# A 65th column of zeros for V's low part, so that all weighing matmuls have one width

## What is computed

```
q = einsum('bsd,dhk->bshk', x, Wq) + bq        # B=2, S=2048, D=256, H=16, K=64
k = einsum('bsd,dhk->bshk', x, Wk) + bk
v = einsum('bsd,dhk->bshk', x, Wv) + bv
scores = einsum('bqhk,bshk->bhqs', q, k) / sqrt(K)
attn = softmax(scores, axis=-1)
ctx = einsum('bhqs,bshk->bqhk', attn, v)
y = x + einsum('bqhk,hkd->bqd', ctx, Wo) + bo
```

## Time and profile before

| | |
|---|---|
| median of 3 runs | 2787.41 us (2786.87 to 2787.42) |
| the profiled execution | 2788.39 us, its span 2786.6 us |
| TensorE | 97% busy, 34,176 matmuls |
| ScalarE | 88% busy |
| VectorE | 84% busy |
| GpSimd | 82% busy |
| first to last weighing matmul | 75.3 to 2415.4 us |

### The profile page before, as it was taken

The page is one execution under the profiler, slowest core; times in us unless marked ns, Lnnn a source line. Parts: engine busy times, 40 slices in busy tenths (PEclk is TensorE's granted clock), DMA queues, the critical chain, the costliest instruction groups (busy, mean ns, idle before and its releaser), DMA issues. The chain is left out here.

```text
span 2786.6 us, 83179 instructions
## 1 busy us (share of the span) xinstructions
PE 2692.4 (97%) x34176; PEld 1723.9 (62%) x34176; DVE 2343.3 (84%) x4203; ACT 2446.4 (88%) x4760; POOL 2274.3 (82%) x1919
## 2 busy tenths in 40 slices
PE   6999999999999999999999999999999999889997
PEld 3566666666666666656666666666666666656664
DVE  6888888999988998768888888898998898578775
ACT  5999999999999999889999999999999999856553
POOL 4898989999999998789899999999999999613233
PEclk9999999999999999999999999999999999999998
DMA  4222222111122222122222122221222212221210
GB/s 133 48 55 57 55 56 73 42 36 35 37 42 42 42 42 42 23 87 55 57 55 53 40 45 42 42 42 42 42 42 42 42 40 83 81 76 46 91 54 23
DMA packets 207100, 144.89 MB, mean 52 GB/s; under 512 B 157824, under 2 KB 181632, under 8 KB 206720
## 3 DMA queue, kind: packets, MB, share of 16 engines
q1 hardware_dynamic: 206720, 139.58, 20.8%
HBM read 51.20 MB, written 37.88 MB: 32 GB/s over the span
## 5 line engine op out<-in xcount | busy, mean ns | idle before, releaser
L554 POOL TENSOR_TENSOR p_l<-p_f,p_h 128x512 f16<-128x512 f32 x1536 | 1946.1, 1295 | 91.0 <-ACT p_h L628 88.2
L681 DVE TENSOR_REDUCE mx<-ps_aux 128x1 f32<-128x512 f32 x2048 | 1349.3, 681 | 298.6 <-PE ps_aux L855 291.3
L627 ACT ACTIVATE p_f<-ps_score 128x512 f32<-128x512 f32 x2048 | 1272.6, 623 | 17.6 <-PE ps_score L884 17.5
L628 ACT ACTIVATE p_h<-ps_score 128x512 f16<-128x512 f32 x2048 | 1283.5, 628 | 0.0
L909 PEld LDWEIGHTS ps_ctx<-v_hi_one_lo,p_h 128*128 128x128 f16 x16384 | 891.3, 97 | 244.9 <-POOL p_l L554 1.2
L909 PE MATMUL ps_ctx<-v_hi_one_lo,p_h 128*128 128x65 f16 (+1 forms) x16384 | 920.9, 194 | 1.1 <-POOL p_l L554 1.0
L909 PE MATMUL ps_ctx<-v_hi_one_lo,p_l 128*128 128x65 f16 x8192 | 791.3, 192 | 0.0
L883 PE MATMUL ps_score<-q_hilo,k_hihi 128*128 128x512 f16 x2048 | 776.9, 379 | 4.7 <-ACT p_h L628 3.4
L884 PE MATMUL ps_score<-q_hi_max,k_lo_one 65*128 65x512 f16 x2048 | 778.6, 380 | 0.0
L855 PE MATMUL ps_aux<-k_hihi,q_hilo 128*128 128x512 f16 x2048 | 621.7, 382 | 15.2 <-DVE xTl L760 7.2
L699 DVE TENSOR_TENSOR p_l<-p_f,p_h 128x512 f16<-128x512 f32 x512 | 538.4, 1052 | 18.6 <-ACT p_h L628 18.6
(11 more groups left out here) (186 smaller groups left out, 2155.2 us busy)
## 6 DMA issues: line engine op xcount, KB each, us to landing
v_heads<-v_new SPq DMA_DIRECT2D x64, 258.0 KB, 2.0
v_hi_one_lo<-v_heads SPq DMA_DIRECT2D x32, 516.0 KB, 6.1
heads<-ctx_n SPq DMA_DIRECT2D x128, 128.0 KB, 2.0
x_all<-heads SPq DMA_DIRECT2D x8, 2048.0 KB, 9.1
k_hihi<-hi_st SPq DMA_DIRECT2D x62, 256.0 KB, 4.4
q_hi_max<-hi_st SPq DMA_DIRECT2D x32, 256.0 KB, 3.5
k_lo_one<-lo_st SPq DMA_DIRECT2D x32, 256.0 KB, 4.3
q_hilo<-hi_st SPq DMA_DIRECT2D x31, 256.0 KB, 3.2
```

What stands on the lines that cost most here:

```text
L554: nc.gpsimd.tensor_tensor(p_l[:, r], p_f[:, r], p_h[:, r], ALU.subtract).then_inc(lo_pool, 1)
L627: nc.scalar.activation(p_f[:, r], ps_score[:, bank], ACT.Exp, scale=exp_scale)
L628: nc.scalar.activation(p_h[:, r], ps_score[:, bank], ACT.Exp, scale=exp_scale).then_inc(exp_done, 1)
L681: nc.vector.reduce_max(mx[:, blk % 2, tt, ch:ch + 1], ps_aux[:, n % SIDE], AX_X).then_inc(max_read, 1)
```

## The change

V's rows get a 130th element, always zero, so that the low part is 65 columns wide as well. The middle matmul of a query tile reads it and writes all 65 columns of the tile's place; the last of them gets zero added. The tiles and the scratch tensor grow by this column (rows of 260 bytes for 258), and VectorE sets the zeros once, at the start. The order of all work, the semaphores and the number of matmuls and DMAs stay.

```
-    VW = 2 * K + 1
+    VW = 2 * K + 2
...
-        V = [sb(f"v_hi_one_lo{u}", [P, KT, VW], F16) for u in range(2)]
+        V = [sb(f"v_hi_one_lo_zero{u}", [P, KT, VW], F16) for u in range(2)]
...
-                nc.gpsimd.tensor_tensor(v_new[:, n % 4, :, K + 1:VW], v_wide[:, n % 2].rearrange("p (h k) -> p h k", k=K),
+                nc.gpsimd.tensor_tensor(v_new[:, n % 4, :, K + 1:VW - 1], v_wide[:, n % 2].rearrange("p (h k) -> p h k", k=K),
                                         v_new[:, n % 4, :, 0:K], ALU.subtract).then_inc(v_ready, 1)
...
             nc.vector.memset(v_new[:, :, :, K:K + 1], 1.0)
+            nc.vector.memset(v_new[:, :, :, VW - 1:VW], 0.0)
...
                     v_one, v_lo = V[u][:, kt, 0:K + 1], V[u][:, kt, K + 1:VW]
-                    parts = [(acc, p_h, v_one), (acc[:, 0:K], p_h, v_lo), (acc, p_l, v_one)]
+                    parts = [(acc, p_h, v_one), (acc, p_h, v_lo), (acc, p_l, v_one)]
...
-    v_scratch = nc.dram_tensor("v_heads", (B, P, S // P, wqk.shape[1], wqk.shape[2] + 1), F16, kind="Internal").ap()
+    v_scratch = nc.dram_tensor("v_heads", (B, P, S // P, wqk.shape[1], wqk.shape[2] + 2), F16, kind="Internal").ap()
```

## The result

| | before | after |
|---|---|---|
| median, 12 runs each | 2787.19 us | 2794.01 us |
| lowest to highest | 2784.54 to 2788.85 | 2792.67 to 2794.94 |
| the profiled execution | 2788.39 us | 2793.41 us |
| its span | 2786.6 us | 2791.6 us |
| first to last weighing matmul | 2340.1 us | 2346.4 us |

The changed kernel is slower: ratio 1.0024, 95% interval 1.0017 to 1.0032, or 6.8 us between the medians. The forecast was 34 us faster, and the time lies outside the range.

The account below looks back on a forecast made before the run. TensorE's own matmul stream was taken as the bound. 31 heads at 1.126 us gave 34.9, less 1 for waits: 34 us off the profiled 2788.39, so 2754.4, or 2753.5 us for the median; range 2746 to 2790.

Parts of the forecast that it names:

- What bounds the kernel: Attention heads: TensorE's own stream sets the pace in 31 heads, 70.8 us a plain head; ScalarE in the last.
- The cost of a 65-column matmul: Weighing stream: 29.0 ns from starts in the longest run, taken as 29.2, leaving 4.4 ns of stall a narrow matmul.
- p_l x2: Timeline group of two 65-column low-probability matmuls, last of one query tile and first of the next; 29.0 ns each.
- the stall: Extra time at each query tile's 64-column middle matmul, taken as 4.4 ns, 8192 times: 36.0 us.
- What is left is its width: Middle matmul: its 64-column width causes the stall, so 65 columns remove it; gain 34 us, chance 0.62.
- The upper end: Middle matmul: the stall stays and a column is added, 0.4 ns at 2.4 GHz or 0.8 by pairs.
- rival 3: Tile's column 64: waiting for the column just written stalls both steps within a tile; 36 us more, 2823, chance 0.07.
- its small form: Middle matmul: the stall stays and the 65th column costs 0.8 ns; 6.7 us more, 2794, chance 0.04.
- Rival 1: Middle matmul: the stall comes with reading V's low part, not the width, and stays; 2787 to 2791, chance 0.20.
- Rival 4: Middle matmul: 64 columns are a cheaper class that the 65th leaves, stall still on top; 2828, chance 0.01.
- The side edits: VectorE's zero memset hidden, V's longer rows about 0.04 us on the first load, GpSimd's row step no cost.
- Rival 5: Plain heads: another engine takes over if it needs over 69.7 us; could cost some us; no separate chance.

Follow-up runs that it names:

- e3: Changed kernel with the middle matmul reading V's high part and the ones again, V's low part left out of the sum; 2779.1 us, ratio 0.9966.
- e6: Kernel before with rows of 136 elements and the low part at element 72, so both parts start on 16 bytes; 2779.5 us, ratio 0.9972.
- e17: Kernel before's widths, rows of 144 elements, high part at element 2, low part at 74, all starts 4 bytes past a 16-byte boundary; 2777.1 us, ratio 0.9962.
- e18: Kernel before's widths, rows of 144 elements, high part at element 1, low part at 73, all starts 2 bytes past a 16-byte boundary; 2788.8 us, ratio 1.0003.
- e1: Changed kernel with the middle matmul back at 64 columns into 64, rows of 130 elements and zeros kept; 2789.0 us, ratio 1.0003.
- e5: Changed kernel with the middle matmul reading V's high part alone, 64 columns into 64, V's low part left out; 2778.7 us, ratio 0.9970.
- e10: e6 with the zero column: rows of 144 elements, low part at element 72, all three matmuls 65 columns wide; 2781.7 us, ratio 0.9984.
- e9: e6 with the middle matmul at 32 columns, half of V's low part left out of the sum; 2768.8 us, ratio 0.9935.
- e16: e6 with the matmul of the low probabilities at 64 columns too, its ones' column left out of the divisor; 2779.4 us, ratio 0.9973.
- e14: e6 with the two matmuls on V's high part 66 columns wide instead of 65, the middle one still 64; 2778.9 us, ratio 0.9967.
- e11: Kernel before's widths, rows of 132 elements, low part at element 66, so every part starts on 4 bytes; 2787.4 us, ratio 1.0002.

## Why the prediction was wrong, point by point

- **What bounds the kernel** held: TensorE's stream in 31 heads. Three heads grew by 0.72 us, and the last head, where TensorE waits for ScalarE, by 0.1 (its 768 weighing matmuls took 59.73 us, now 59.83).
- **The cost of a 65-column matmul, 29.0 to 29.2 ns, failed.** It was read from the gaps behind two of the six matmuls of a period ("p_l x2"), in a stream where the others pay for them. The steady cost is 30.2 ns (e3). My own other bound, 29.8 from the projections, was nearer and I passed it over because a row showed "the very instruction". With 30.2 the period of 184 ns leaves (184 - 181)/2 = 1.5 ns a tile for the stall, so even with the right cause the gain would have been 12 us and not 34.
- **"What is left is its width", the step that set the sign, failed.** I had ruled out the place in the bank, the weights and the change of the moving tensor, and was left with width or position in the row; rows could not part them. I gave width 0.62 because everything of equal widths ran without a stall. But the streams it was read from had either no change of source ("p_l x2") or 512 columns; the comparison with 512 columns had no power, as 2 ns in a gap of 216 vanish in rows that go by 10 ns. In its place: the stall comes with where the operands start, odd elements and different places within 16 bytes (e6, e17, e18), and it stays when the width changes (the changed kernel). The widths were to bring 34 us; they took 6.8, and equal starts with the widths of before (e17) gave 10.
- **The upper end, "a column is added, 0.4 ns at 2.4 GHz or 0.8 by pairs", was what happened:** 0.73 ns by e1, 0.94 ns for the whole change. It stood in rival 3 as its small form, 2794 us at 0.04, and the time came out at 2794.0. That it fits to the tenth is luck: the column accounts for 6 us of the 6.8 (8192 x 0.73 ns), the wider row for the rest. The size is right; as a mechanism it is only partly so, since the same column costs 0.16 ns on the high part (e5) and 0.49 on aligned rows (e10).
- **Rival 1** (the stall comes with reading V's low part) was right about the stall, which it put down to the low part's place in the row or the step back after it, but priced the column at 0 to 0.4 ns, 2787 to 2791.
- **Rival 4 and the Trainium skill's figures** ("TensorE: Matmul & The Clock Gate", section on the back-to-back issue gap): the gap of N/2.4 plus 2.5 ns, which the section gives for matmuls with no weight loads between them (here each has one), gives 29.6 ns at 65 columns, and the steady stream has 30.2. It has about 25 ns for anything up to 64 columns; here 32 columns took 26.6 (e9), but 64 beside 65 were worth 0.16 to 0.73 ns and not 4.6.
- **The side edits held:** the memset is 0.09 us in the shadow of the load, V's DMAs land as before, GpSimd's busy time is the same (2273.2 for 2274.3 us). The row of 260 bytes, which I had at nothing for the matmuls, goes with 0.16 us more by three heads (e1 against before). That is the one place where a layout edit touched the matmuls, and it is not explained: in e1 fewer of them start odd than before.
- **Rival 5**, another engine only above 67.8 us a head, was too easy: at 70.0 to 71.0 TensorE already waits for VectorE (e9), and at 70.4 now and then (e16, e17), so busy times of others do not say where the next limit is.

## What to carry to other kernels

A gap between two neighbours' starts in a pipelined stream need not be the cost of the first; take whole periods, and take the steady cost from a long stream of one form. When rows leave two causes that always come together, no count of agreeing rows decides between them: bound the gain by both, or vary one alone. And for short matmuls (some 65 columns) look first at where in memory the moving operand starts: even elements, and the same place within 16 bytes from one matmul to the next, gave 8 to 10 us of 2787 here, by padding a row (e17: 0.9962, interval 0.9949 to 0.9974; e14 and e6 alike), where the zero column lost 7.

## What the hardware showed that I had not expected

- The start of a moving float16 operand matters below 16 bytes: 2777.1 us with all starts 4 bytes past a boundary, 2788.8 with all 2 bytes past one, 2785.7 with starts at 0 and 8.
- Halving a matmul from 64 to 32 columns shortened the period of six, two of them halved, from 181 to 170 ns (e6, e9), 5 to 6 ns for each; its own place in the stream is still 26.6 ns.
- 66 columns in all three (2790.3 us) beat 65 in all three (2794.0), for all that they stream three columns more a tile. The two kernels differ in the low part's start too, so this alone does not convict the odd count, and 66 columns took longer than 65, 64 and 65 on the same rows (e11, 2787.4).
- Left open: by what mechanism an odd start, an odd count and a change of place interact. The costs don't add up simply (e18, with odd starts alone, loses as much as the kernel before, which has both, and as e1, where only the low part starts odd but the places differ), and no row shows the inside of the read.
